# Gated attention after cross-attention on one core: VectorE also turns the odd heads' probability tiles in five of eight rounds, and small products and counts move to GpSimd and ScalarE

## The chip, the cores and the metric

One core of a Trainium2 chip. The metric is the device time of one launch in microseconds (us), given as the median over several runs. TensorE is PE in the rows, VectorE DVE, ScalarE ACT, GpSimd POOL, and SyncE, which issues the transfers, SP.

## The reference, cut to what matters

Two layers over x of shape 8 x 512 x 512 (batch, tokens, width). The first, a cross-attention, gives x1. The second, in which the change lies, works on the normalised x1:

```python
q = (x @ Wq)  # 8 heads of 64;  k = (x @ Wk) likewise
wv = topk_mask(x @ Ws, 2) * sigmoid(x @ Ws)     # per token, head, expert (5)
xv = einsum('btd,edk->btek', x, Wv)
v = einsum('bthe,btek->bhtk', wv, xv)           # values, mixed over experts
probs = softmax(q * scale @ k.T)                # 512 x 512 per head
attn = probs @ v
mask_o = topk_mask(x @ Wd, 2)
out = einsum('bthe,bthk,ekd->btd', mask_o, attn, Wo)
x = x1 + tanh(g) * out
```

## The kernel before, in words

The program has five instruction streams, one per engine, written out by hand; each engine runs its stream in order and waits on semaphores. The second layer (from about 490 us on) takes one batch after another, and a batch goes through **rounds**, numbered n. Rounds 0 to 7 make the scores: heads come in pairs p (an even and an odd one), a pair has two rounds, and a round has four score tiles of 128 queries x 512 keys, in the order even, odd, even, odd head. Preparation of a batch lies in rounds -3 to -1, and its end in rounds 8 to 12. Since a batch's round n + 8 is the next batch's round n, the loop over batches (`Fori`) runs rounds 5 to 12 of batch b, woven with rounds -3 to 4 of batch b + 1. Below, a round is called by its number 5 to 12 in the loop's body; 8 to 12 are then the next batch's 0 to 4.

Within a round each engine goes through the places SCORES, BEFORE, TURNS, BEHIND, AFTER. The table `AT` says at which round and place a unit of matrix work stands: "q", "k", "experts", "turn_y" (transposes of the normalised input), "values" (probs @ v), "turn_o" (turns attn back), "turn_z", "result". All these but "values" share three PSUM banks (`RING`) in the order of the list: a unit waits until the unit three places ahead of it has been read (`wait_bank`, `wait_read`); for "turn_o" of pair p this is when both `mix_product`s of the pair are done.

A score tile goes this way. TensorE makes it (`scores`, L2251); VectorE takes the row maximum (`row_max`, L1860); ScalarE takes the exponential into SBUF (`scores_exp`, L1670). For "values" the tile must be turned. An **even** head's tile is turned in 32 x 32 blocks by VectorE (`turn_blocks`, L1865), and then SP issues four transfers that put the blocks in place in `pt` (`move_blocks`, L1519). An **odd** head's tile is turned by TensorE (`turn_probs`, L2259: four transposes against an identity) and copied from PSUM by ScalarE (`probs_copy`, L1679).

GpSimd mixes the values of each pair (`mix_values`, L1587 and L1593: five products and four sums of 128 x 512) and adds some heads' expert products (`mix_sums`, L1605). Its stream in the loop is `mix_sums(b, 2)`, `mix_values(b + 1, 0)`, then `rest(b + 1)`: the values of pairs 1, 2, 3, and then `mix_sums` of pairs 0 and 1. VectorE makes the products of the attention output with the output gates (`mix_product`, L1879), two heads each in rounds 5, 7, 9 and 10, which need `coef`, the gates over the softmax sums (`coefficients`, L1903, VectorE, rounds 11, 5, 7 and 8). VectorE also ranks the logits in round 8 (`compare`, `count_better`, L1948 to L1960) and copies the norm values (`take_norm`, L1856). `route_values` (round 9) turns the ranks into `pick` and `mask`; `pick` starts the next batch's `mix_values`.

```python
                if a == 0:
                    dve.wait_ge(to_ps, b * PAIRS + p + 1)
                    dve.wait_ge(coef_ready, b * PAIRS + p + 1)
```

These lines head `mix_product`. The last batch ends outside of the loop, in `last_rounds`, where TensorE turns all tiles.

Of the kernel before, what the change touches and what calls it, by code (L numbers as in the profile page):

```python
# [24 lines left out]
ALU = mybir.AluOpType  # L25
# [3 lines left out]
P = 128  # L29
# [1138 lines left out]
def expert_attention(nc, block, both, x1, g_ffn, wk, wo, out):  # L1168
# [29 lines left out]
    BANKS = 4  # L1198
# [32 lines left out]
    COEFFICIENTS_AT = (3, 5, 7, 8)  # L1231
# [38 lines left out]
    with ExitStack() as mem:  # L1270
# [36 lines left out]
        probs_odd = sb("probs_odd", [P, BANKS // 2, T])  # L1307
# [32 lines left out]
        compared = sem("compared")  # L1340
        gates = sem("gates")
# [21 lines left out]
        coef_ready = sem("coef_ready")  # L1363
        z_dve = sem("z_dve")
# [54 lines left out]
        def even_probs(n):  # L1419
            return probs_even[:, n // BANKS % 2, :, n % BANKS // 2, :]  # L1420

        def plain_probs(n):

            if n % 2:
                return probs_odd[:, n % BANKS // 2, :]
            return both.tmp[:, n // BANKS % 2 * 2 + n % BANKS // 2, :]
# [50 lines left out]
        COMPARISONS, GATES = 2 * (E - 1), E + 1  # L1477
# [5 lines left out]
        ODD_STEPS, ODD_ROUND = STEPS // 2, BANKS // 2  # L1483
        MOVED = QUADS * 16
        LAST_TURNED = (B - 1) * ODD_STEPS + (CUT + 1) * ODD_ROUND - (CUT + 1) * BANKS

        def odd_turned(b, n):

            return b * ODD_STEPS + n // 2 + 1

        def all_turned(n):

            return LAST_TURNED + n + 1

# [4 lines left out]
        def _(sp):  # L1499
# [11 lines left out]
            def move_blocks(b, r, first=False):  # L1511

                p = r // 2
                sp.wait_ge(blocks_turned, b * ODD_STEPS + (r + 1) * ODD_ROUND)
                if first and p == 2:

                    sp.wait_ge(o_ps, p - 1)
                for q in range(QUADS):
                    sp.dma_start(by_rows(2 * p % 4)[:, r % 2, q].rearrange("p k s a -> p (k s a)"),  # L1519
                                 probs_even[q * BLOCK:(q + 1) * BLOCK, r % 2].rearrange(  # L1520
                                     "p (j k) s a -> p j (k s a)", j=QUADS)).then_inc(moved[r % 2], 16)
# [43 lines left out]
        def _(pool):  # L1565
# [68 lines left out]
            pool.wait_ge(coef_ready, B * PAIRS)  # L1634
# [5 lines left out]
        def _(act):  # L1640
# [8 lines left out]
            def normalise(b, tiles):  # L1649
                act.wait_ge(norm_ready, b)  # L1650
                act.wait_ge(x1_loaded, b * 16)
# [3 lines left out]

            def scores_exp(b, n, first):
                act.wait_ge(nmax_ready, b * STEPS + n + 1)
                h, t = head_tile(n)
                scores = ps_s[:, n % BANKS, :]
                if n % 2 == 0:  # L1660
                    if n >= 2 * BANKS or not first:

                        act.wait_ge(moved[n // BANKS % 2], (b * PAIRS + n // PAIR) * MOVED)
                    out, scores = even_probs(n), scores.rearrange("p (j a) -> p j a", a=BLOCK)
# [8 lines left out]
            def probs_copy(b, n, first):  # L1673
                h, t = head_tile(n)
                act.wait_ge(pt_ps, odd_turned(b, n))
                if t == 0 and (h >= 4 or not first):

                    act.wait_ge(o_ps, b * PAIRS + h // 2 - 1)
                act.activation(turned(n), scored(n), ACT.Copy).then_inc(pt_ready, 1)  # L1679

            def last_exp(b, n):
                act.wait_ge(nmax_ready, b * STEPS + n + 1)
                h, t = head_tile(n)
                if n % 2 == 0:
                    act.wait_ge(moved[n // BANKS % 2], (b * PAIRS + n // PAIR) * MOVED)
                elif n < STEPS - BANKS:
                    act.wait_ge(pt_ps, odd_turned(b, n - BANKS))
                else:
                    act.wait_ge(pt_ps, all_turned(n - BANKS))
# [55 lines left out]
            def step(b, n, place, first=False):  # L1745
# [18 lines left out]
                elif place == TURNS:  # L1764
# [3 lines left out]
                    if 0 <= n < ROUNDS:  # L1768
# [72 lines left out]
        def _(dve):  # L1841
# [10 lines left out]
            def take_norm(b):  # L1852

                dve.wait_ge(last_newton, ROOT_STEPS + 1)
                dve.wait_ge(y_act, b * NT)
                dve.tensor_scalar(norm[:], x1_norm[:, :, bass.ds(b * NT, NT)], 1.0, None, ALU.mult).then_inc(norm_ready, 1)  # L1856

# [606 lines left out]
```

## Time and profile before

| what | value |
|---|---|
| median of 3 runs | 1152.17 us (1152.14 to 1153.83) |
| the profiled execution | 1152.18 us, span 1150.4 us |
| busy, TensorE | 97% of the span |
| busy, VectorE | 79% |
| busy, ScalarE | 51% |
| busy, GpSimd | 57% |
| granted TensorE clock | 1.00 |

The span goes from the first instruction to the last; 1.8 us lie around it. Busy shares are means over two layers. A row of the timeline reads: start in us, length in us, engine, line, operation, what it writes from what it reads, how many instructions are merged, and in brackets how long the engine was idle before them and what ended the wait.

### The profile page before, as it was taken

How to read it: one execution, taken by the hardware profiler on the slowest of the kernel's cores; microseconds unless marked ns; L12 is line 12 of the kernel's file. 1: busy time of each engine (PE TensorE's matmuls, PEld its weight loads, DVE VectorE, ACT ScalarE, POOL GpSimd, SP SyncE). 2: the span in 40 equal slices, each digit the busy share in tenths (PEclk: the TensorE clock that was granted, in tenths of full speed). 3: DMA queues.
4: the chain of work that ended last, by engine and by line, in shares of the span. 5: the costliest groups of instructions: out<-in, count | busy, mean ns of one | idle time of the engine just before them, and what ended most of it. 6: DMA issues, size and time to landing. Idle time of an engine off the chain costs nothing.

```text
span 1150.4 us, 19136 instructions
## 1 busy us (share of the span) xinstructions
PE 1120.2 (97%) x5885; PEld 856.2 (74%) x5885; DVE 904.9 (79%) x1656; ACT 588.6 (51%) x1332; POOL 658.0 (57%) x476
## 2 busy tenths in 40 slices
PE   7999999999999999999999999999999999999998
PEld 6888888888888888886666767767667666767655
DVE  7998787878787866578597797786887876976977
ACT  7634443434444344447455555555556545565543
POOL 2645252525252524329759579389398498496694
DMA  5441414141414132343324323324225233242241
GB/s 202 147 138 46 138 46 128 55 128 55 128 55 128 55 91 92 129 129 74 91 56 129 88 51 117 91 55 130 71 58 161 55 91 111 55 122 59 55 128 38
DMA packets 76606, 108.44 MB, mean 94 GB/s; under 512 B 7712, under 2 KB 40224, under 8 KB 76576
## 3 DMA queue, kind: packets, MB, share of 16 engines
q1 hardware_dynamic: 76576, 108.07, 31.0%
q8 instruction: 15, 0.25, 0.1%
q14 instruction: 15, 0.12, 0.0%
HBM read 58.76 MB, written 16.78 MB: 66 GB/s over the span
## 4 chain that ended last, share of the span: by engine, by line
PE 68%; POOL 13%; DVE 8%; issue 6%; ACT 4%; DVEq 0%; DMA 0%; POOLq 0%; ACTq 0%; SPq 0%
PE ps_f L992 23%; PE ps_s L992 8%; PE ps_o L2274 7%; PE ps_h L992 7%; POOL spare L1587 6%; PE ps_r L2200 6%; POOL spare L1593 5%; PE ps_r L2233 5%; PE ps_s L2251 4%; PE ps_r L2209 3%; DVE nmax L1860 3%; PE ps_s L2259 2%; DVE z_tmp L1879 2%; ACT probs_odd L1670 1%; POOL z L1605 1%
## 5 line engine op out<-in xcount | busy, mean ns | idle before, releaser
L1860 DVE TENSOR_REDUCE nmax<-ps_s 128x1 f32<-128x512 f32 x256 | 158.5, 680 | 79.0 <-PE ps_s L2251 78.0
L1587 POOL TENSOR_TENSOR spare<-xv,pick 128x512 f32<-128x512 f32 x160 | 184.8, 1155 | 35.0 <-DVE pick L1975 22.1
L1605 POOL TENSOR_TENSOR z<-z,z_tmp 128x1280 f32<-128x1280 f32 x35 | 102.6, 2932 | 138.6 <-DVE z_tmp L1879 136.3
L1593 POOL TENSOR_TENSOR spare<-spare 128x512 f32<-128x512 f32 x128 | 165.6, 1294 | 10.0
L1670 ACT ACTIVATE tmp<-ps_s,nmax 128x512 f32<-128x512 f32 x124 | 85.2, 687 | 97.1 <-DVE nmax L1860 97.1
L2274 PE MATMUL ps_o<-pt,spare 128*64 128x512 f32 x496 | 113.3, 598 | 6.6 <-POOL spare L1593 5.1
L254 POOL TENSOR_TENSOR e_t<-e_t 128x512 fp32r<-128x512 f32 x28 | 35.4, 1300 | 135.7 <-ACT e_t L510 135.7
L2251 PE MATMUL ps_s<-k,q 64*128 64x512 f32 x768 | 106.4, 408 | 3.1 <-ACT pt L1679 3.1
L2251 PEld LDWEIGHTS ps_s<-k,q 64*128 64x128 f32 x768 | 67.3, 184 | 49.3 <-issue 33.3
L254 POOL TENSOR_TENSOR c<-stage,c 128x512 fp32r<-128x512 f32 x28 | 42.3, 1542 | 94.4 <-ACT c L250 94.4
L2200 PE MATMUL ps_r<-es_t,c_t 128*128 128x512 f32 x384 | 96.3, 399 | 0.0
L2200 PE MATMUL ps_r<-es_t,wk 128*128 128x512 f32 x384 | 95.2, 397 | 0.0
L992 PE MATMUL ps_s<-c_t,es_t 128*128 128x512 f32 x384 | 92.8, 393 | 2.4 <-DVE es_t L727 2.4
L992 PE MATMUL ps_f<-wec,e_t 128*128 128x512 f32 x384 | 92.1, 392 | 0.0
L992 PE MATMUL ps_f<-weh,eh_t 128*128 128x512 f32 x384 | 91.9, 391 | 0.0
L992 PE MATMUL ps_f<-wh,h_t 128*128 128x512 f32 x384 | 91.3, 390 | 0.5 <-DVE h_t L887 0.5
L992 PE MATMUL ps_h<-es_t,c 128*128 128x512 f32 x384 | 88.7, 390 | 0.2 <-DVE es_t L781 0.2
L1670 ACT ACTIVATE probs_odd<-ps_s,nmax 128x512 f32<-128x512 f32 x124 | 85.1, 686 | 0.0
L992 PEld LDWEIGHTS ps_s<-c_t,es_t 128*128 128x128 f32 x384 | 71.0, 188 | 17.8 <-DVE es_t L727 2.8
L992 PEld LDWEIGHTS ps_f<-wh,h_t 128*128 128x128 f32 x384 | 72.0, 188 | 15.9 <-DVE h_t L887 0.9
L992 PEld LDWEIGHTS ps_h<-es_t,c 128*128 128x128 f32 x384 | 71.9, 188 | 15.1 <-DVE es_t L781 0.3
L992 PEld LDWEIGHTS ps_f<-wec,e_t 128*128 128x128 f32 x384 | 71.4, 188 | 15.0 <-DVE wec L254 0.4
(245 smaller groups left out, 2272.2 us busy)
## 6 DMA issues: line engine op xcount, KB each, us to landing
pt<-tmp SPq DMA_DIRECT2D x248, 128.0 KB, 2.6
stage<-in_x SPq DMA_DIRECT2D x32, 256.0 KB, 3.2
x_sb<-in_x SPq DMA_DIRECT2D x8, 1024.0 KB, 5.3
x_dram<-x_sb SPq DMA_DIRECT2D x32, 256.0 KB, 3.1
stage<-x_dram SPq DMA_DIRECT2D x8, 1024.0 KB, 5.4
x_sb<-x_dram SPq DMA_DIRECT2D x8, 1024.0 KB, 5.4
out_dram<-x_sb SPq DMA_DIRECT2D x31, 256.0 KB, 2.6
stage<-in_ctx_t SPq DMA_DIRECT2D x28, 256.0 KB, 2.8
```

Source lines behind the costliest of these rows:

```text
L254: return eng.tensor_tensor(pair[:, 1, k, :], operand[:, k, :], pair[:, 0, k, :].bitcast(F32), ALU.subtract)
L992: last = pe.matmul(out, left(l, k), right(r, k), start=start and n == 1, stop=stop and n == ND * len(PASSES))
L1587: pool.tensor_tensor(v_tmp[:] if e else acc, xv[:, :, e, :].unsqueeze(2).broadcast_to(shape), pick[:, e, :, 2 * p:2 * p + 2].unsqueeze(3). ...
L1593: pool.tensor_tensor(acc, acc, v_tmp[:], ALU.add).then_inc(v_steps, 1)
L1605: pool.tensor_tensor(zv, zv, z_tmp[:, h % 2], ALU.add).then_inc(z_pool, 1)
L1670: act.activation(out, scores, ACT.Exp, bias=nmax[:, n:n + 1], accum_out=den[:, h, t:t + 1]).then_inc(p_exp, 1)
L1860: dve.tensor_reduce(nmax[:, n:n + 1], ps_s[:, n % BANKS, :], AX_X, ALU.max, negate=True).then_inc(nmax_ready, 1)
L2200: end = pe.matmul(ps, w2[:, l, k, n * P:(n + 1) * P], y_t2[:, r, k, :], start=m == 0, stop=m == len(every) - 1)
L2209: end = pe.matmul(ps[:, 0:NX], y_t2[:, l, k, n * P:(n + 1) * P], wx2[:, r, k, :], start=m == 0, stop=m == len(every) - 1)
L2233: end = pe.matmul(ps, z_t2[:, zt(l, k), n * P:(n + 1) * P], wo2[:, r, k, :], start=m == 0, stop=m == len(every) - 1)
L2251: end = pe.matmul(ps_s[:, (n + a) % BANKS, :], q2[head_rows(a), p % 2, l, t * P:(t + 1) * P], k2[head_rows(a), p % 2, r, :], start=m == 0, ...
L2274: end = pe.matmul(ps_o[head_rows(a), :], v_acc[:, p, k, a, :], rows, start=k == 0, stop=k == NT - 1)
```

## The change

`ALL_BY_VECTOR` names rounds 0, 4, 5, 6 and 7. In these rounds VectorE turns both heads' tiles, in one instruction for the two tiles of a head (128 x 1024), SP moves both heads' blocks (eight transfers in place of four), and TensorE's transposes and ScalarE's copies of the odd tiles fall away; TensorE's next scores wait for the exponentials there, not for the copies. The odd tiles have two places now, as the even ones.

`coefficients` leaves VectorE for GpSimd (but pairs 2 and 3 of the last batch). It stands in GpSimd's stream between the mixtures: pair 0 behind `mix_values` of pair 2, pair 1 behind `mix_values` of pair 3, pair 2 behind `mix_sums` of pair 1, pair 3 ahead of `mix_sums` of pair 2. The four adds of `count_better` become `rank` on GpSimd, which stands ahead of that. ScalarE makes the copy of the norm values.

```diff
-    COEFFICIENTS_AT = (3, 5, 7, 8)
+
+    ALL_BY_VECTOR = (0, 4, 5, 6, 7)
...
-        probs_odd = sb("probs_odd", [P, BANKS // 2, T])
+        probs_odd = sb("probs_odd", [P, BANKS // 2, T])[:], spare[:, 1, 2:4, :]
...
+        def blocks(r, i):
+
+            if i:
+                return probs_odd[r % 2].rearrange("p s t -> p (s t)").rearrange("p (j s a) -> p j s a", s=2, a=BLOCK)
+            return probs_even[:, r % 2]
...
+                for i in heads_moved(r):
+                    sp.wait_ge(blocks_turned, b * tiles_moved(ROUNDS) + tiles_moved(r) + 2 * i + 2)
+                    if first and p == 2 and i == 0:
+
+                        sp.wait_ge(o_ps, p - 1)
+                    for q in range(QUADS):
+                        sp.dma_start(by_rows((2 * p + i) % 4)[:, r % 2, q].rearrange("p k s a -> p (k s a)"),
+                                     blocks(r, i)[q * BLOCK:(q + 1) * BLOCK].rearrange(
+                                         "p (j k) s a -> p j (k s a)", j=QUADS)).then_inc(moved[r % 2], 16)
...
+            def coefficients(b, p):
+                heads = slice(2 * p, 2 * p + 2)
+                pool.wait_ge(rden_ready, b * PAIRS + p + 1)
+                if p == 0:
+                    pool.wait_ge(mask_ready, b + 1)
+                pool.tensor_tensor(coef[:, heads], mask[:, :, :, heads].rearrange("p e t h -> p h t e"),
+                                   rden[:, heads, :].unsqueeze(3).broadcast_to([P, 2, NT, E]),
+                                   ALU.mult).then_inc(coef_ready, 1)
+
+            def rank(b):
+
+                pool.wait_ge(compared, (b + 1) * COMPARISONS)
+                rows = beaten[:].rearrange("p s k j g -> p (s k) j g")
+                pool.tensor_tensor(better[:], rows[:, :, 0, :], rows[:, :, 1, :], ALU.add).then_inc(ranked, 1)
+                for j in range(2, E - 1):
+                    pool.wait_ge(ranked, b * RANKS + j - 1)
+                    pool.tensor_tensor(better[:], better[:], rows[:, :, j, :], ALU.add).then_inc(ranked, 1)
+                pool.wait_ge(sig_exp, b + 1)
+                pool.wait_ge(ranked, b * RANKS + RANKS - 1)
+                pool.tensor_tensor(logits[:].rearrange("p s k g -> p (s k) g"), better[:], rows[:, :, E - 1, :],
+                                   ALU.add).then_inc(ranked, 1)
+
             def rest(b, first=False):
-                for p in range(1, PAIRS):
-                    mix_values(b, p, first)
+                mix_values(b, 1, first)
+                mix_values(b, 2, first)
+                coefficients(b, 0)
+                mix_values(b, 3, first)
+                coefficients(b, 1)
                 for p in range(LAST_PAIR - 1):
                     mix_sums(b, p)
+                coefficients(b, 2)
...
+            def turn_of(b):
+
+                rank(b + 1)
+                coefficients(b, LAST_PAIR)
+                mix_sums(b, LAST_PAIR - 1)
+                mix_values(b + 1, 0)
+
+            rank(0)
             mix_values(0, 0, True)
             rest(0, True)
             with pool.Fori(0, B - 2) as b:
-                mix_sums(b, LAST_PAIR - 1)
-                mix_values(b + 1, 0)
+                turn_of(b)
                 rest(b + 1)
-            mix_sums(B - 2, LAST_PAIR - 1)
-            for p in range(PAIRS):
-                mix_values(B - 1, p)
+            turn_of(B - 2)
+            mix_values(B - 1, 1)
+            mix_values(B - 1, 2)
+            coefficients(B - 1, 0)
+            mix_values(B - 1, 3)
+            coefficients(B - 1, 1)
...
+                if tiles[0] == 0:
+                    act.wait_ge(last_newton, ROOT_STEPS + 1)
+                    act.activation(norm[:], x1_norm[:, :, bass.ds(b * NT, NT)], ACT.Copy).then_inc(norm_ready, 1)
...
+            def place_free(b, n, first):
+
+                r = n // BANKS
+                if first and r < 2:
+                    return
+                if n % BANKS == 0:
+                    act.wait_ge(moved[r % 2], moved_through(b, r - 2))
+                elif n % 2 not in heads_moved((r - 2) % ROUNDS):
+                    act.wait_ge(pt_ps, odd_turned(b, n - 2 * BANKS))
...
+                if n % 2 in heads_moved(r):
+                    out, scores = blocks(r, n % 2)[:, :, n % BANKS // 2, :], scores.rearrange("p (j a) -> p j a", a=BLOCK)
                 else:
-                    if n >= BANKS or not first:
-
-                        act.wait_ge(pt_ps, odd_turned(b, n - BANKS))
-                    out, scores = plainly(probs_odd[:, n % BANKS // 2, :]), scores_by_keys(scores)
+                    out, scores = plainly(plain_probs(n)), scores_by_keys(scores)
...
+                    if 0 <= n < ROUNDS and n not in ALL_BY_VECTOR:
                         for tile in range(n * BANKS + 1, n * BANKS + BANKS, 2):
                             probs_copy(b, tile, first)
...
-            def turn_blocks(b, n):
-
-                dve.wait_ge(p_exp, b * STEPS + n + 1)
-                dve.transpose(even_probs(n), even_probs(n)).then_inc(blocks_turned, 1)
+            def turn_blocks(b, r, i):
+
+                dve.wait_ge(p_exp, b * STEPS + r * BANKS + i + 3)
+                both_tiles = blocks(r, i).rearrange("p j s a -> p (j s a)")
+                dve.transpose(both_tiles, both_tiles).then_inc(blocks_turned, 2)
...
-            def coefficients(b, p):
+            def last_coefficients(b, p):
                 heads = slice(2 * p, 2 * p + 2)
                 dve.wait_ge(rden_ready, b * PAIRS + p + 1)
-                if p == 0:
-                    dve.wait_ge(mask_ready, b + 1)
                 dve.tensor_tensor(coef[:, heads], mask[:, :, :, heads].rearrange("p e t h -> p h t e"),
                                   rden[:, heads, :].unsqueeze(3).broadcast_to([P, 2, NT, E]),
-                                  ALU.mult).then_inc(coef_ready, 1)
+                                  ALU.mult).then_inc(last_coef, 1)
...
-            def count_better(b):
-
-                dve.wait_ge(compared, (b + 1) * COMPARISONS)
-                rows = beaten[:].rearrange("p s k j g -> p (s k) j g")
-                dve.tensor_tensor(better[:], rows[:, :, 0, :], rows[:, :, 1, :], ALU.add).then_inc(gates, 1)
-                for j in range(2, E - 1):
-                    dve.wait_ge(gates, b * GATES + j - 1)
-                    dve.tensor_tensor(better[:], better[:], rows[:, :, j, :], ALU.add).then_inc(gates, 1)
+            def count_values(b):
                 dve.wait_ge(sig_exp, b + 1)
-                dve.wait_ge(gates, b * GATES + E - 2)
-                dve.tensor_tensor(logits[:].rearrange("p s k g -> p (s k) g"), better[:], rows[:, :, E - 1, :],
-                                  ALU.add).then_inc(gates, 1)
-
-            def count_values(b):
                 dve.tensor_scalar(sig[:], sig[:], 1.0, None, ALU.add).then_inc(gates, 1)
...
+                dve.wait_ge(ranked, b * RANKS + RANKS)
...
-                        for tile in range(n * BANKS, n * BANKS + BANKS, 2):
-                            turn_blocks(b, tile)
+                        for i in heads_moved(n):
+                            turn_blocks(b, n, i)
...
-                    pe.wait_ge(pt_ready, odd_turned(b, n + 1 - BANKS))
+                    if (n // BANKS - 1) % ROUNDS in ALL_BY_VECTOR:
+                        pe.wait_ge(p_exp, b * STEPS + n + 2 - BANKS)
+                    else:
+                        pe.wait_ge(pt_ready, odd_turned(b, n + 1 - BANKS))
...
-                pe.wait_ge(pt_ready, odd_turned(b, PAIR * p + PAIR - 1))
-                for r in range(2):
-                    pe.wait_ge(moved[r], (b * PAIRS + p + 1) * MOVED)
+                if not {2 * p, 2 * p + 1} <= set(ALL_BY_VECTOR):
+                    pe.wait_ge(pt_ready, odd_turned(b, PAIR * p + PAIR - 1))
+                for r in (2 * p, 2 * p + 1):
+                    pe.wait_ge(moved[r % 2], moved_through(b, r))
...
+                    elif place == TURNS and n not in ALL_BY_VECTOR:
                         for tile in range(n * BANKS + 1, n * BANKS + BANKS, 2):
                             turn_probs(b, tile)
```

## Rows read from the trace of the kernel before

**Rows 1.** The page, part 1: busy us, share of the span and instructions.

```profile
PE 1120.2 (97%) x5885; PEld 856.2 (74%) x5885; DVE 904.9 (79%) x1656; ACT 588.6 (51%) x1332; POOL 658.0 (57%) x476
```

**Rows 2.** One period of the loop, rounds 5 to 12: length, busy time by engine.

```profile
700.91:782.12 81.21, 79.46 (x446) 56.37 (x445) 64.75 (x102) 45.96 (x113) 58.48 (x42) 1.00 0.32 90
```

**Rows 3.** The chain that ended last, in order of time, from round 9.

```profile
749.34 1.29 POOL z L1605
...
768.55 3.65 PE ps_o L2274 x16
```

**Rows 4.** Timeline of TensorE, rounds 5 to 7.

```profile
707.64 0.65 PE L2191 MATMUL ps_r<-ident,stage 128*128 128x128 f32 x4 [0.40 <-DVE z_tmp L1879]
...
716.50 1.03 PE L2259 MATMUL ps_s<-ident,probs_odd 128*128 128x128 f32 x8
717.66 4.58 PE L2209 MATMUL ps_r<-c,es_t 128*128 128x400 f32 x24
...
729.75 1.04 PE L2259 MATMUL ps_s<-ident,probs_odd 128*128 128x128 f32 x8
730.72 3.65 PE L2274 MATMUL ps_o<-pt,spare 128*64 128x512 f32 x16
```

**Rows 5.** Timeline of GpSimd, rounds 9 to 7 of the next period.

```profile
749.33 5.92 POOL L1605 TENSOR_TENSOR z<-z,z_tmp 128x1280 f32<-128x1280 f32 x2 [16.15 <-DVE z_tmp L1879]
...
758.84 2.17 POOL L1587 TENSOR_TENSOR spare<-xv,pick 128x512 f32<-128x512 f32 x1
...
762.47 1.05 POOL L1587 TENSOR_TENSOR spare<-xv,pick 128x512 f32<-128x512 f32 x1
...
778.38 1.29 POOL L1593 TENSOR_TENSOR spare<-spare 128x512 f32<-128x512 f32 x1
...
789.57 1.28 POOL L1593 TENSOR_TENSOR spare<-spare 128x512 f32<-128x512 f32 x1
```

**Rows 6.** Timeline of VectorE, round 9, and rounds 12 and 5.

```profile
747.68 2.88 DVE L1879 TENSOR_TENSOR z_tmp<-ps_r,coef 128x1280 f32<-128x1280 f32 x2
...
778.37 1.30 DVE L1865 STREAM_TRANSPOSE tmp<-tmp 128x512 f32<-128x512 f32 x2
...
785.82 1.48 DVE L1879 TENSOR_TENSOR z<-ps_r,coef 128x1280 f32<-128x1280 f32 x1
```

**Rows 7.** Groups of the second layer: busy us, mean ns, idle before.

```profile
L1865 DVE STREAM_TRANSPOSE tmp<-tmp 128x512 f32<-128x512 f32 x124 | 80.1, 682 | 0.0
...
L1903 DVE TENSOR_TENSOR coef<-mask,rden 128x40 f32<-128x40 bf16 x32 | 22.9, 716 | 0.0
...
L1957 DVE TENSOR_TENSOR better<-better,beaten 128x320 bf16<-128x320 bf16 x16 | 5.2, 325 | 0.6
```

**Rows 8.** Timeline of the first batch, round 5: GpSimd, VectorE, and TensorE's round 7.

```profile
546.26 1.27 POOL L1593 TENSOR_TENSOR spare<-spare 128x512 f32<-128x512 f32 x1
...
540.03 1.48 DVE L1879 TENSOR_TENSOR z<-ps_r,coef 128x1280 f32<-128x1280 f32 x1
...
559.75 1.67 PE L2251 MATMUL ps_s<-k,q 64*128 64x512 f32 x12 [2.08 <-ACT pt L1679]
```

**Rows 9.** Timeline of TensorE at the start of the program.

```profile
4.07 4.08 PE L999 MATMUL ps_b<-ident 128*128 128x128 f32 x18 [4.07 <-DVE stats L663]
...
9.79 1.04 PE L999 MATMUL ps_b<-ident 128*128 128x128 f32 x8
```

**Rows 10.** Timeline of the last batch: VectorE, SP's queue, TensorE, GpSimd.

```profile
1110.28 1.48 DVE L1879 TENSOR_TENSOR z<-ps_r,coef 128x1280 f32<-128x1280 f32 x1
...
1115.42 2.50 SPq L1519 DMA_DIRECT2D pt<-tmp  x4
...
1120.07 3.65 PE L2274 MATMUL ps_o<-pt,spare 128*64 128x512 f32 x16 [1.53 <-issue]
...
1128.86 1.95 PE L2301 MATMUL ps_o<-pt,spare 128*64 128x256 f32 x16 [0.84 <-issue]
...
1137.68 1.54 POOL L1619 TENSOR_TENSOR z<-z,pt 128x640 f32<-128x640 f32 x1 [2.85 <-DVE z L2056]
```

More of the change, by code:

```diff
@@ L1474, in head_rows, with heads_moved, tiles_moved, odd_tiles @@
             return slice(a * DH, a * DH + DH)
-        COMPARISONS, GATES = 2 * (E - 1), E + 1
+        COMPARISONS, RANKS, GATES = 2 * (E - 1), E - 1, 2
         V_STEPS = 2 * E - 1
-        ODD_STEPS, ODD_ROUND = STEPS // 2, BANKS // 2
-        MOVED = QUADS * 16
-        LAST_TURNED = (B - 1) * ODD_STEPS + (CUT + 1) * ODD_ROUND - (CUT + 1) * BANKS
+        def heads_moved(r):
+            return range(2 if r in ALL_BY_VECTOR else 1)
+        def tiles_moved(r):
+            return sum(2 * len(heads_moved(i)) for i in range(r))
+        def odd_tiles(n):
+            return sum(m // BANKS not in ALL_BY_VECTOR for m in range(1, n + 1, 2))
+        def transfers(r):
+            return sum(QUADS * 16 * len(heads_moved(i)) for i in range(r % 2, r + 1, 2))
+        def moved_through(b, r):
+            earlier = r < 0
+            return b * transfers(ROUNDS - 2 + r % 2) + transfers(r + ROUNDS * earlier) - earlier * transfers(
+                ROUNDS - 2 + r % 2)
         def odd_turned(b, n):
-            return b * ODD_STEPS + n // 2 + 1
+            earlier = n < 0
+            return b * odd_tiles(STEPS - 1) + odd_tiles(n + STEPS * earlier) - earlier * odd_tiles(STEPS - 1)
         def all_turned(n):
-            return LAST_TURNED + n + 1
+            return (B - 1) * odd_tiles(STEPS - 1) + odd_tiles((CUT + 1) * BANKS - 1) + n + 1 - (CUT + 1) * BANKS
         POOL_SUMS, LAST_PAIR = H - 3, PAIRS - 1
@@ L1513, in move_blocks @@
                 p = r // 2
[L1514 to L1521, printed above, removed]
+                for i in heads_moved(r):
[6 more added lines that the diff above has]
+                                         "p (j k) s a -> p j (k s a)", j=QUADS)).then_inc(moved[r % 2], 16)
             def steady(b, more):
@@ L1658, in scores_exp @@
                 h, t = head_tile(n)
[L1659 to L1664, printed above, removed]
-                else:
-                    if n >= BANKS or not first:
-                        act.wait_ge(pt_ps, odd_turned(b, n - BANKS))
-                    out, scores = plainly(probs_odd[:, n % BANKS // 2, :]), scores_by_keys(scores)
+                r, scores = n // BANKS, ps_s[:, n % BANKS, :]
+                place_free(b, n, first)
+                if n % 2 in heads_moved(r):
+                    out, scores = blocks(r, n % 2)[:, :, n % BANKS // 2, :], scores.rearrange("p (j a) -> p j a", a=BLOCK)
+                else:
+                    out, scores = plainly(plain_probs(n)), scores_by_keys(scores)
                 act.activation(out, scores, ACT.Exp, bias=nmax[:, n:n + 1],
@@ L1675, in probs_copy @@
                 act.wait_ge(pt_ps, odd_turned(b, n))
-                if t == 0 and (h >= 4 or not first):
+                if n % BANKS == 1 and (h >= 4 or not first):
                     act.wait_ge(o_ps, b * PAIRS + h // 2 - 1)
@@ L1683, in last_exp @@
                 h, t = head_tile(n)
[L1684 to L1689, printed above, removed]
+                place_free(b, n, False)
                 act.activation(plainly(plain_probs(n)), scores_by_keys(ps_s[:, n % BANKS, :]), ACT.Exp, bias=nmax[:, n:n + 1],
@@ L1985, in step @@
                 if place == SCORES:
-                    if n == NORMALISE_AT and not first:
-                        take_norm(b)
                     for p in range(PAIRS):
@@ L2080, in last_rounds @@
                     row_max(b, n)
-                coefficients(b, 2)
+                last_coefficients(b, 2)
                 for h in (2, 3):
@@ L2088, in last_rounds @@
                 row_sums(b, 3)
-                coefficients(b, 3)
+                last_coefficients(b, 3)
                 last_mix(5, turned_pair(2))
@@ L2246, in scores @@
                 elif n >= BANKS or not first:
-                    pe.wait_ge(pt_ready, odd_turned(b, n + 1 - BANKS))
+                    if (n // BANKS - 1) % ROUNDS in ALL_BY_VECTOR:
+                        pe.wait_ge(p_exp, b * STEPS + n + 2 - BANKS)
+                    else:
+                        pe.wait_ge(pt_ready, odd_turned(b, n + 1 - BANKS))
                 for m, (l, r) in enumerate(PASSES):
```

25 lines of the change are left out of this document (9 added, 16 removed).

## The prediction

> **What bounds the kernel now.** I read the busy shares first, then the chain that ended last, then the timelines of one period. TensorE is busy 97% of the span, and in a period of the second layer 79.5 of 81.2 us [rows 1, 2]. So five rounds without its transposes look like pure gain. The chain says something else beside it: in round 9 it enters GpSimd's sums, stays on GpSimd over the whole mixture of pair 0, and comes back to TensorE when "values" of pair 0 may start, 19 us later [rows 3]. GpSimd is busy only 58.5 of the 81.2 us [rows 2], but between round 9 and round 7 its stream has no free time. Whatever is queued into that stretch is paid in full by whoever waits for it. The second thing to see is that TensorE's second turn_y of round 5 waits 0.40 us for VectorE's products [rows 4]: it needs the bank that `mix_product` of heads 0 and 1 must have read. TensorE has no lead over these products.
>
> **The change, part by part.**
>
> *TensorE.* The turning of a round's two odd tiles takes, from its start to the next unit's, 1.16 us in round 6 and 0.97 in round 7 [rows 4]; I take 1.0 for the others. Five rounds are 5.0 us a period; 38 rounds are changed in all (8 batches by 5, less rounds 6 and 7 of the last), 38 us.
>
> *VectorE.* Two more tiles cost 1.3 us a round (0.68 each, 1.30 for two) [rows 6, 7], 6.5 us a period. Four coefficients at 0.72 [rows 7], four counts at 0.33 or a little more [rows 7], together 4.3 us, and a small norm copy go. Net some +2 us on 64.8 busy of 81.2 [rows 2]: it is covered by VectorE's waits.
>
> *ScalarE* loses ten copies and gains one tiny one; at 46 of 81 us busy [rows 2] it doesn't matter.
>
> *GpSimd, coefficients.* This is the step that decides. `coefficients(b, 0)` now stands behind `mix_values` of pair 2. In the timeline of before, the stream that starts with the sums at 749.33 ends the mixture of pair 2 at 789.57 + 1.28 = 790.85 [rows 5]. But VectorE uses this coefficient at 785.82, in round 5 [rows 6]. It will wait. The price of the coefficient itself is not in the trace: GpSimd takes 1.54 us for 640 elements and 2.9 for 1280 [rows 5, 10], so 2.1 ns an element and 0.2 fixed, which gives 0.3 us for 40; bounds are 0.1 (elements alone) and 1.05 (a whole product of 512). With 0.1 to issue it and 0.2 for the signal to VectorE, as from VectorE to GpSimd (the second product of round 9 starts half way through the 2.88 us from 747.68, and so the first ends at 749.12; the sums start at 749.33) [rows 5, 6] product 0 starts at 791.4 instead of 785.8: **5.6 us late**, 4.9 us if the coefficient is free, 6.4 if dear.
>
> Nothing hides it. VectorE stands at product 0, behind it the low part of k for pair 3, the round's block turns and all later row maxima; TensorE stands at the second turn_y. GpSimd's stretch starts with the products of round 9, so this is a closed loop. From the end of round 9's first product (749.12) to product 0: 36.7 us before, 42.3 after. From product 0 to the first product's end in round 9: 749.12 - (785.82 - 81.2) = 44.5 us before [rows 2, 6]. Of that, round 6 gives 1.16 and round 7 gives 0.97; round 8 is VectorE's (it trades 0.2 of coefficient and 1.5 of counts for 1.3 of turns), so 0.4 to 0.5. The savings of rounds 12 and 5 (some 0.85 each) lie ahead of the wait and only make it longer. Period: 42.3 + 44.5 - 2.6 = 84.2, **3.0 us more than before** (81.2), not 5.0 less.
>
> *GpSimd, counts.* Four adds of 320 by the same line are 0.85 each, with gaps 3.9 us, while VectorE has some 4.4 us of other work between the comparisons and `pick` (four row maxima, the low part of q, the reciprocal). I cost it at nothing. At the price of a whole 512 (1.29) [rows 5] it would be about 1 us late, and with a dear coefficient behind it, which `mask` waits for, 2 us a period. The Trainium skill, GPSIMD Engine Reference, section Engine selection, says that elementwise work belongs on VectorE, GpSimd being about twice as slow; by that factor on the trace's 0.325 us the four adds take 2.6 us and are hidden too.
>
> *Port.* When VectorE adds two SBUF operands, a GpSimd product takes 2.17 us for the usual 1.05; beside VectorE's block turns a GpSimd sum keeps its 1.29 [rows 5, 6]. So I add nothing for more turns beside the mixtures. If they did collide, two such rounds would lie in the stretch, 2 to 4 us a period. The Trainium skill, SBUF — State Buffer, section Who interferes with whom, has the same line between one SBUF input and two.
>
> *Transfers.* Eight in place of four a round: four are issued in 2.50 us, and "values" starts 2.15 us after the last [rows 10]. In the loop a round is 8 to 12 us and `pt` is needed a round or more later, so it is hidden; if it weren't, 2.5 us a round. At the end it isn't hidden (below).
>
> *TensorE after the wait.* TensorE reaches the second turn_y earlier by rounds 12 and 5 and waits longer: 5.6 + 0.4 + 1.7, so 7.7 us in one piece. The trace has one wait that long or near it, 4.07 us at the program's start, and behind it 18 transposes take 4.08 us (0.227 each), where 8 later take 1.04 (0.130), though the granted clock reads 1.00 in all rows; a wait of 2.08 us in the first batch slows nothing (12 score products 1.67 us) [rows 8, 9]. The start may be slow for another reason. I take it as the same thing, since 7.7 is well past 4.07: 4.08 - 18 x 0.130 = **1.74 us** lost behind each such wait, on the path. With none it is 0; with half speed through the following "values" (3.65 us) as well, 3.6. The Trainium skill, TensorE: Matmul & The Clock Gate, Part 1, says that an idle TensorE falls from 2.4 to 1.2 GHz and must be busy again before it gets the clock back; by that rule the loss is certain, which speaks against this change.
>
> *The ends.* First batch: the mixture of pair 2 ends at 547.53, product 0 stood at 540.03 [rows 8], so 8.1 us late; less 1.0 for round 0's turning, ahead of it. Less 2.6 as above and 2.1, because TensorE's wait in round 7 (2.08, which came from the end of the mixtures) goes: +2.4 us. Last batch: 5.6 late, then "values" of pair 2 wait for round 5's eight transfers. Product 0 to "values" was 1120.07 - 1110.28 = 9.8; it becomes 2.8 + 0.6 + 1.2 (products, k, first turn) + 5.0 + 2.15 = 11.8: +2.0; and 0.84 of wait for the last mixture goes [rows 10]: +6.8.
>
> *Sum.* 2.4 + 6 periods x 3.0 + 6.8 = 27.2; eight slow restarts x 1.74 = 13.9; together 41 us on the profiled execution's 1152.2 (span 1150.4 and 1.8 around it), which is the median too. **1193 us.**
>
> **The rivals.**
>
> *Clock stays (22%).* The start is slow for its own reason. Then 1152.2 + 27.2 = 1179.
>
> *GpSimd's small work is dear (12%).* Counts and coefficient at the upper bounds, 2.3 us more a period: 7 x 2.3 = 16, so 1209. For it: no row has a GpSimd operation of this size or of bf16. Against: the line through 640 and 1280 has a small fixed part.
>
> *The wait is partly absorbed (9%).* The mixtures run faster with fewer two-input operations of VectorE beside them (the two 2.17 us products at 1.05 would give 2.2 us a period), and TensorE's clock stays: 1179 - 7 x 2.2 = 1164; up to a third of this case comes out within 0.2% of 1152.
>
> *Faster (8%).* The late coefficient holds VectorE only, and TensorE runs on through the order of the banks, so that its own work sets the time: 1152 - 38 = 1114. It needs the wait at product 0 to cost the loop less than the 2.6 us that rounds 6, 7 and 8 give back. Against it are the 0.40 us wait at turn_y and that the product is read in place from one of three banks. For it: TensorE's 97%.
>
> *Worse than all (4%):* round 9 and the transfers add to the wait, 1215 or more.
>
> The forecast with waits and slow restarts has 45%.
>
> **Range and chances.** 1172 to 1210 takes in the clock rival, the bounds of the coefficient (5 us each way) and the dear case to its centre. A difference under 0.2% can't be told from none here. Slower 45 + 22 + 12 + 6 + 4 = 89%, same 3%, faster 8%.
>
> **What the changed profile would show.** VectorE's product 0 in round 5 idle before by several us, released by GpSimd's coefficient; TensorE idle before the second turn_y of every round 5, 7 to 8 us, released by product 1; periods of 84 us (86 with slow restarts, and then longer "values" behind the wait); GpSimd's mixtures unchanged; ranks done before `pick`. Wrong would be: product 0 without idle time, periods under 81, counts over 1 us each, or turns that stretch GpSimd's products.

## The result, and the profile after

The changed kernel takes **1205.6 us** (median of 4 runs, 1204.2 to 1205.9) beside 1152.7 of the kernel before on the same chip: ratio 1.0456, 95% interval 1.0441 to 1.0472. It is slower, as forecast; 1193 was forecast, with a range of 1172 to 1210.

The busy row and the row of the granted clock of its page, beside [rows 1]:

```profile
PE 1106.2 (92%) x5581; PEld 828.6 (69%) x5581; DVE 911.5 (76%) x1563; ACT 553.2 (46%) x1263; POOL 689.0 (57%) x538
PEclk9999999999999999997998998999989989989989
```

TensorE has 304 matmuls less to do and is 14 us less busy, in a span 54 us longer: it waits. Here are TensorE, VectorE and GpSimd in round 5, the place of [rows 4, 6]; each fence is one engine's timeline.

```profile
719.02 0.66 PE L2234 MATMUL ps_r<-ident,stage 128*128 128x128 f32 x4 [0.67 <-ACT stage L1716]
726.48 1.11 PE L2234 MATMUL ps_r<-ident,stage 128*128 128x128 f32 x4 [6.81 <-DVE z_tmp L1937]
727.52 6.15 PE L2321 MATMUL ps_o<-pt,spare 128*64 128x512 f32 x16
```
```profile
723.47 1.49 DVE L1937 TENSOR_TENSOR z<-ps_r,coef 128x1280 f32<-128x1280 f32 x1 [6.62 <-POOL coef L1636]
```
```profile
721.75 1.26 POOL L1617 TENSOR_TENSOR spare<-spare 128x512 f32<-128x512 f32 x1
723.09 0.27 POOL L1636 TENSOR_TENSOR coef<-mask,rden 128x40 f32<-128x40 bf16 x1
723.32 2.18 POOL L1611 TENSOR_TENSOR spare<-xv,pick 128x512 f32<-128x512 f32 x2
```

Read it from the bottom. A coefficient of 0.27 us stands behind the last sum of a mixture of 11 us (712.02 to 723.01). VectorE's product 0 has waited 6.62 us for it, and TensorE's second turn_y 6.81 us for the second product of VectorE. And the "values" behind that wait take 6.15 us where they take 3.65 in [rows 4]. The windows of this stretch (length; busy time of TensorE, its loads, VectorE, ScalarE, GpSimd; then the granted clock) say why:

```profile
719.00:723.00 4.00, 0.66 (x4) 0.42 (x4) 0.00 (x0) 3.04 (x5) 3.77 (x4) 0.92 0.54 208
723.00:725.00 2.00, 0.00 (x0) 0.00 (x0) 1.53 (x2) 0.00 (x0) 1.84 (x4) 0.50 0.64 190
...
729.00:731.00 2.00, 2.00 (x8) 0.48 (x5) 1.51 (x4) 0.00 (x0) 1.84 (x3) 0.50 0.60 145
731.00:733.00 2.00, 2.00 (x8) 0.61 (x6) 0.00 (x0) 0.00 (x0) 1.84 (x3) 0.60 0.78 202
733.00:735.00 2.00, 2.00 (x16) 1.05 (x12) 0.40 (x1) 0.60 (x1) 1.92 (x3) 1.00 0.69 177
```

During the wait the granted clock falls from 1.00 to 0.50, from 2.4 to 1.2 GHz, and it is back only when "values" are nearly done. It does so in all eight batches, and these "values" take 4.6 to 6.2 us. (By the Trainium skill, TensorE: Matmul & The Clock Gate, Part 1, this had to follow an idle stretch; the trace agrees, with 0.92 in the stretch in which TensorE stops and 0.50 in the next.)

GpSimd's new small work in round 8 answers [rows 7]:

```profile
763.55 0.79 POOL L1644 TENSOR_TENSOR better<-beaten 128x320 bf16<-128x320 bf16 x1 [8.35 <-DVE beaten L2004]
764.42 1.67 POOL L1647 TENSOR_TENSOR better<-better,beaten 128x320 bf16<-128x320 bf16 x2
766.17 0.79 POOL L1650 TENSOR_TENSOR logits<-better,beaten 128x320 f32<-128x320 bf16 x1
...
769.89 2.92 POOL L1629 TENSOR_TENSOR z<-z,z_tmp 128x1280 f32<-128x1280 f32 x1 [2.69 <-DVE z_tmp L1937]
```

The counts end at 766.96 and `pick` starts at 767.80, so they are hidden, and GpSimd waits another 2.69 us before its sums. The end, beside [rows 10] (TensorE, then SyncE's queue). TensorE waits twice. The first wait is for the low part of k, which VectorE writes behind its products until 1164.90; the second is for round 5's transfers:

```profile
1165.00 2.93 PE L2297 MATMUL ps_s<-k,q 64*128 64x512 f32 x12 [4.92 <-issue]
...
1173.26 5.15 PE L2321 MATMUL ps_o<-pt,spare 128*64 128x512 f32 x16 [4.28 <-issue]
```
```profile
1166.08 2.50 SPq L1543 DMA_DIRECT2D pt<-tmp  x4
1168.63 2.58 SPq L1543 DMA_DIRECT2D pt<-spare  x4
```

**Where the 53.6 us of span went.** Product 0 of round 5 marks each batch. Before it starts at 540.03 in the first batch, at 623.42 in the second and at 1110.28 in the last; after at 547.44, 635.34 and 1161.41. The first batch is 7.4 us later there, the first period 4.5 us longer (83.4 to 87.9), the six periods of the loop 39.2 us (81.1 to 87.7 each, +6.5), and the stretch from the last product 0 to the end 2.5 us (40.1 to 42.6). The forecast in the same parts is 7.1, 2.6, 28.4 and 2.9.

### The profile page after: what moved, and what is told of

It reads as the page before. It is cut to its first block, busy times and chain, and to the rows that moved or that the text cites. A ratio compares the mean times of both kernels' runs of the same rounds, so it can differ in the third digit from the quotient of the medians.

```text
span 1204.0 us, 18434 instructions
## 1 busy us (share of the span) xinstructions
PE 1106.2 (92%) x5581; PEld 828.6 (69%) x5581; DVE 911.5 (76%) x1563; ACT 553.2 (46%) x1263; POOL 689.0 (57%) x538
## 4 chain that ended last, share of the span: by engine, by line
PE 57%; POOL 21%; DVE 10%; issue 7%; ACT 3%; POOLq 1%; DVEq 0%; DMA 0%; ACTq 0%; SPq 0%
PE ps_f L992 22%; POOL spare L1611 11%; POOL spare L1617 9%; PE ps_s L992 7%; PE ps_h L992 6%; PE ps_o L2321 6%; PE ps_r L2243 4%; PE ps_r L2252 3%; PE ps_s L2297 3%; DVE nmax L1917 2%; DVE z_tmp L1937 2%; ACT probs_odd L1738 1%; POOL z L1629 1%; DVE beaten L2004 1%; ACT tmp L1738 1%
## 5 line engine op out<-in xcount | busy, mean ns | idle before, releaser
L1738 ACT ACTIVATE tmp<-ps_s,nmax 128x512 f32<-128x512 f32 x124 | 85.4, 688 | 120.3 <-DVE nmax L1917 120.3
L2321 PE MATMUL ps_o<-pt,spare 128*64 128x512 f32 x496 | 127.4, 661 | 9.4 <-POOL spare L1617 5.1
L2297 PEld LDWEIGHTS ps_s<-k,q 64*128 64x128 f32 x768 | 68.4, 186 | 52.5 <-issue 39.6
L2321 PEld LDWEIGHTS ps_o<-pt,spare 128*64 128x64 f32 x496 | 36.4, 152 | 81.8 <-issue 75.0
L2252 PE MATMUL ps_r<-c,es_t 128*128 128x400 f32 x384 | 75.3, 348 | 7.0 <-DVE es_t L1969 7.0
```

The source lines that it names most:

```text
L1738: act.activation(out, scores, ACT.Exp, bias=nmax[:, n:n + 1], accum_out=den[:, h, t:t + 1]).then_inc(p_exp, 1)
L2252: end = pe.matmul(ps[:, 0:NX], y_t2[:, l, k, n * P:(n + 1) * P], wx2[:, r, k, :], start=m == 0, stop=m == len(every) - 1)
L2297: end = pe.matmul(ps_s[:, (n + a) % BANKS, :], q2[head_rows(a), p % 2, l, t * P:(t + 1) * P], k2[head_rows(a), p % 2, r, :], start=m == 0, ...
L2321: end = pe.matmul(ps_o[head_rows(a), :], v_acc[:, p, k, a, :], rows, start=k == 0, stop=k == NT - 1)
```

## The experiments

All stand beside the kernel before on the same chip, and each compares with the changed kernel unless told otherwise. The table has the time, its ratio with the interval, the mean of the six loop periods and the first one (product 0 to product 0), and the time from the last product 0 to the end.

| kernel | median us | ratio to before | period | first | end |
|---|---|---|---|---|---|
| before | 1152.7 | | 81.1 | 83.4 | 40.1 |
| after | 1205.6 | 1.0456 (1.0441 to 1.0472) | 87.7 | 87.9 | 42.6 |
| x1 early coefficient | 1139.8 | 0.9885 (0.9869 to 0.9902) | 78.8 | 82.8 | 45.9 |
| x2 TensorE kept busy | 1193.2 | 1.0341 (1.0324 to 1.0358) | 85.4 | 87.3 | 44.4 |
| x3 no odd turns | 1210.2 | 1.0499 (1.0482 to 1.0517) | 88.6 | 88.2 | 39.6 |
| x4 turns only | 1153.3 | 1.0004 (0.9994 to 1.0013) | 80.6 | 82.5 | 45.1 |
| x5 = x1, counts on VectorE | 1155.0 | 1.0011 (1.0001 to 1.0021) | 80.6 | 81.6 | 45.9 |
| x6 = x1, all eight rounds | 1162.2 | 1.0075 (1.0058 to 1.0092) | 81.9 | 83.2 | 45.4 |
| x7 = x1, no odd turns | 1159.4 | 1.0047 (1.0030 to 1.0063) | 81.1 | 86.9 | 45.6 |
| x8 = x1, rounds 0, 4, 7 | 1149.8 | 0.9966 (0.9952 to 0.9981) | 79.8 | 86.0 | 45.9 |
| x9 = x1, rounds 0, 4, 6, 7 | 1140.5 | 0.9890 (0.9874 to 0.9907) | 78.7 | 83.1 | 47.3 |

(x1's parts are those of its repetition x11: 1139.1 us, 0.9881, 0.9864 to 0.9897. In x1's own profiled execution they are 78.7, 81.5 and 46.1. Each row's parts are of one execution, so a difference of 1 us in "first" says nothing. That of x9 took 1.9 us more than its median.)

**x1, the order alone.** `coefficients(b, 0)` goes one mixture earlier, in the loop and in the last batch:

```diff
                 mix_values(b, 1, first)
+                coefficients(b, 0)
                 mix_values(b, 2, first)
-                coefficients(b, 0)
                 mix_values(b, 3, first)
```

> The changed kernel with one thing moved: GpSimd makes the coefficients of pair 0 behind the mixture of pair 1, not of pair 2. If the late coefficient is the cause, product 0 of round 5 no longer waits, TensorE's 6.8 us wait in round 5 and the slow stretch behind it go, and the next limit is the end of GpSimd's mixtures (experts of the next batch may be written only then): a period of 77 to 78 us in place of 88.4, total 1120 to 1132. If the turns on VectorE or the eight transfers are the cause, the time stays near 1205.

Measured 1139.8, 66 us less than after and 13 less than before; the period is 78.8. The cause is as expected; the time is 8 us above the expected 1120 to 1132. TensorE in round 5:

```profile
699.60 1.41 PE L2234 MATMUL ps_r<-ident,stage 128*128 128x128 f32 x8 [0.67 <-ACT stage L1716]
700.93 3.65 PE L2321 MATMUL ps_o<-pt,spare 128*64 128x512 f32 x16
...
710.37 4.59 PE L2252 MATMUL ps_r<-c,es_t 128*128 128x400 f32 x24 [1.00 <-DVE es_t L1969]
```

The 6.8 us wait is gone and so is the slow stretch. The whole loss was the place of one 0.27 us instruction. What misses of the expected gain stands in the same rows, 0.67 us behind ScalarE's casts and 1.00 at the low part of y (`es_t`), and at the end, where 45.9 us follow the last product 0 instead of 40.1. TensorE waits there 6.50 us for round 5's transfers (first row, the timeline of x11), and it is tempting to name these. The chain of x11 at that place (second fence: start, length, what) says otherwise:

```profile
1106.61 6.04 PE L2321 MATMUL ps_o<-pt,spare 128*64 128x512 f32 x16 [6.50 <-issue]
```
```profile
1108.81 1.05 POOL spare L1611
...
1109.93 1.28 POOL spare L1617
...
1111.28 0.28 POOL coef L1636
...
1111.65 0.10 DVE z_tmp L2078
```

VectorE waits 7.81 us for the last batch's `coefficients(B - 1, 1)`, behind the mixture of pair 3: the same fault a second time, one pair later. It lies over the wait for transfers. In the loop nothing else took the coefficient's place: the chain of x11 goes from round 9's products over GpSimd's sums and the mixture of pair 0 to "values" (978.70 to 997.95, 19.2 us), as in [rows 3].

**x2, the wait without the fall of the clock.** TensorE does 56 transposes that nobody reads while it would wait:

```diff
+                if (name, n) == ("turn_y", 1):
+                    pe.wait_ge(p_exp, b * STEPS - STEPS + (CUT + 1) * BANKS)
+                    for _ in range(56):
+                        pe.transpose(ps_s[:, 0, 0:P], ident[:], ident[:])
```

> The changed kernel with 56 idle transposes on TensorE (0.11 us each, 6.2 us, into a score bank that is free) ahead of the second turn_y of round 5, where it waits 6.8 us for product 0. The wait itself stays. If the slow values (5.4 to 6.2 us for 3.65) behind it come from the idle time, they go back to 3.65, the granted clock is 1.00 again, and 7 periods get 2.5 to 3 us shorter: 1184 to 1190, a little less if the 1.0 us wait at experts goes too. If they come from something else (the transfers, the turns), the time stays at 1205 or gets worse.

Measured 1193.2, a gain as expected and 3 us short of its range. VectorE's wait is still 6.61 us, but the granted clock is 1.00 from 715 to 730 and behind the idle work "values" take 3.65 again:

```profile
716.10 6.28 PE L2233 MATMUL ps_s<-ident 128*128 128x128 f32 x56
723.06 0.65 PE L2238 MATMUL ps_r<-ident,stage 128*128 128x128 f32 x4 [0.68 <-DVE z_tmp L1937]
723.64 3.65 PE L2325 MATMUL ps_o<-pt,spare 128*64 128x512 f32 x16
```

So of the 6.5 us that a period has more, the low clock is 2.3 (87.7 less 85.4) and the rest, 4.3, is the late product less what the turns give. The first and the last batch have waits that the idle work doesn't fill (3.98 us behind it in the first), and stayed slow: "values" take 5.09 and 6.42 us there.

**x3, without the turns.** `ALL_BY_VECTOR = ()`, all else as in the change.

> The changed kernel without its turns: no round is turned by VectorE alone; coefficients and counts stay on GpSimd and the norm copy on ScalarE, at the changed places. If the moves alone set the time, product 0 waits as in the changed kernel (about 5.6 us), TensorE idles about 6 us and is slow behind it: a period of 88 to 90 us, 1200 to 1215. If the turns have a part in the loss, it lies clearly under 1200; if they are the whole loss, at 1150.

Measured 1210.2, period 88.6, as the first case has it:

```profile
727.23 1.11 PE L2234 MATMUL ps_r<-ident,stage 128*128 128x128 f32 x4 [5.87 <-DVE z_tmp L1937]
728.27 5.10 PE L2321 MATMUL ps_o<-pt,spare 128*64 128x512 f32 x16
```

The wait belongs to the moved coefficient and not to VectorE's turns or the transfers. Under the late coefficient the turns are worth 0.9 us a period (88.6 to 87.7). The 1.0 us wait for the low part of y, once a batch in the changed kernel (7.0 us in seven waits), does not exist here, so it comes with the turns; x9 shows with which.

**x4, the turns alone.** Coefficients and counts back on VectorE, where they were; the norm copy stays on ScalarE.

```diff
+    COEFFICIENTS_AT = (3, 5, 7, 8)
...
             def coefficients(b, p):
+                return
...
             def rank(b):
 
+                return
...
+                    if n in COEFFICIENTS_AT:
+                        coefficients(b, COEFFICIENTS_AT.index(n))
...
                         compare(b)
+                        count_better(b)
```

The two returns empty GpSimd's functions; VectorE has its own again.

> The turns alone: odd heads' tiles on VectorE in five rounds and the norm copy on ScalarE as changed, but coefficients and counts back on VectorE at their old places. If the turns are worth their 5 us of TensorE a period where nothing waits for GpSimd, the period is limited by the longer VectorE work of round 8 and by GpSimd's mixtures: about 79 us, 1130 to 1140. If VectorE becomes the bound (67 to 70 us of work) or the transfers hold up, 1150 or more.

Measured 1153.3, no difference from before: **the expected 1130 to 1140 was wrong**, and its other case, VectorE as the bound, came out. TensorE is busy 4 us a period less than before (75.39 us from 702.75 to 783.33, against 79.46 in [rows 2]), but the period is only 0.5 shorter. VectorE waits for nobody from 736 to 762, in rounds 8 and 9, where the counts lie:

```profile
736.93 1.20 DVE L1926 STREAM_TRANSPOSE probs_odd<-probs_odd 128x1024 f32<-128x1024 f32 x1
738.05 1.93 DVE L2016 TENSOR_TENSOR beaten<-logits 128x256 bf16<-128x256 f32 x8
740.01 0.33 DVE L2022 TENSOR_TENSOR better<-beaten 128x320 bf16<-128x320 bf16 x1
740.37 0.68 DVE L2025 TENSOR_TENSOR better<-better,beaten 128x320 bf16<-128x320 bf16 x2
```

Its row maxima come late, so do ScalarE's exponentials, and TensorE waits at its odd tiles in round 9 (timeline, the same place one period on):

```profile
825.18 0.66 PE L2332 MATMUL ps_s<-ident,spare 128*128 128x128 f32 x4 [1.17 <-ACT spare L1741]
826.52 0.73 PE L2332 MATMUL ps_s<-ident,spare 128*128 128x128 f32 x4 [0.68 <-ACT spare L1741]
827.19 5.22 PE L2348 MATMUL ps_o<-pt,spare 128*64 128x512 f32 x16
```

Here nothing lies over the transfers at the end, and the chain shows 6.46 us of waiting for them and then "values" of 5.54 us: product 0 to the end is 5 us longer than before, and that eats what the loop gave.

**x5, x1 with the counts back on VectorE** (`rank` empty, `count_better` behind `compare`; the coefficients stay on GpSimd).

> Coefficients of pair 0 made early on GpSimd, turns as changed, and the four counts back on VectorE (1.5 us in round 8, ahead of pick, mask and product 4). If round 8 and 9 of VectorE are on the loop that sets the period, each period grows from 78.75 by about 1.5 us to 80.2: 1148 to 1152. If the counts on GpSimd were hidden either way, nothing changes: 1140.

Measured 1155.0, 3 us above the expected range, and the period is 80.6, as in x4. Beside x1 the counts on GpSimd are worth 1.8 us a period and 15 us in all. x4 and x5 differ in who makes the coefficients, and the period is the same: moving these is worth nothing here, although the coefficients are 0.86 us each on VectorE in x4. TensorE's waits for the exponentials of the odd tiles, in x5 (first) and in x11 (second; us in total, times, longest):

```profile
PE ps_s L2319 <- ACT spare L1739: 16.7, 20, 1.4
```
```profile
PE ps_s L2305 <- ACT spare L1738: 6.4, 15, 0.6
```

A count takes GpSimd 0.79 us and VectorE 0.33 [rows 7], and still it belongs on GpSimd, which waits at that place, while VectorE has nothing free. (The Trainium skill, GPSIMD Engine Reference, section Engine selection, puts elementwise work on VectorE because GpSimd is about twice as slow; the price agrees with the runs, 0.79 to 0.33, the advice does not hold in a round where VectorE is full.)

**x6, x1 with all eight rounds by VectorE.** `ALL_BY_VECTOR = (0, 1, ..., 7)`.

> Coefficients of pair 0 early on GpSimd, and all eight rounds turned by VectorE. TensorE loses another 3 us of work a period, VectorE gains 3.6 us in rounds 9 to 11, where it has hardly a wait. If TensorE's work set the period it would fall to 76 and the total to 1120. If the loop over VectorE's round 9 and GpSimd's mixture of pair 0 sets it, the period stays within 1 us of 78.75: 1135 to 1147.

Measured 1162.2, **wrong again**, above both of its cases, for the same reason: in rounds 9 and 10 VectorE has no wait left, and its sum of z comes late to turn_z. TensorE's waits for it:

```profile
PE ps_r L2266 <- DVE z L1948: 35.6, 7, 5.1
```

**x7, x1 with no odd turns.** `ALL_BY_VECTOR = ()`.

> Coefficients of pair 0 early on GpSimd, counts on GpSimd, norm copy on ScalarE, and no round turned by VectorE alone: the moves without the turns. VectorE has 4.3 us less a period, 1.7 of it in round 8 where it led TensorE by little. If that is on the loop, the period falls from 81.2 to about 80.3: 1144 to 1148; the turns are then worth 1.5 us a period, of the 5.0 that TensorE is spared. If the moves are worth nothing by themselves, 1152.

Measured 1159.4, above both cases, period 81.1: the moves alone are worth nothing in the loop. What is lost lies in the first batch (86.9) and at the end (45.6, though TensorE waits but 1.2 us for transfers here; the chain runs over GpSimd's mixtures and the late coefficient as in x1). In the first batch ScalarE waits with the logits until the last mixture is done, and the copies of round 6's odd tiles stand behind them; with round 6 turned by VectorE no copy is there. ScalarE, then TensorE:

```profile
558.86 0.24 ACT L1788 ACTIVATE logits<-ps_r 128x80 f32<-128x80 f32 x1 [7.16 <-POOL spare L1617]
...
559.32 1.09 ACT L1747 ACTIVATE pt<-ps_s 128x512 f32<-128x512 f32 x2
```
```profile
559.97 2.93 PE L2297 MATMUL ps_s<-k,q 64*128 64x512 f32 x12 [3.37 <-ACT pt L1747]
```

**x8, x1 with rounds 0, 4 and 7.** It was to keep the gain and spare the end its transfers.

> Coefficients of pair 0 early on GpSimd, and only rounds 0, 4 and 7 turned by VectorE. In round 6 TensorE's saving of 1.16 us is followed by a wait of 1.0 for the low part of y, in round 5 its 0.87 by a wait of 0.67 for ScalarE, so turning these two back costs about 0.4 us a period; at the end of the last batch the wait for round 5's transfers (6.5 us) and the slow values behind it (2.9 us) go. Sum: 1140 + 3 - 8 = 1135, 1130 to 1138. If the turns of rounds 5 and 6 do pay in full, 1145 or more.

Measured 1149.8, far from the expected 1135, as in the case that the turns pay in full: the first period is 86.0, close to x7's, each loop period 1.1 longer than x1's, and the end is as long as x1's although round 5 moves half the blocks there. With x7 it says that fewer transfers don't shorten x1's end. The loop period grows by what x7 showed in the first batch: TensorE's scores wait for ScalarE's copies of round 6 (some 1.0 us a period, 4.4 in the first batch), which stand behind the logits and so behind GpSimd's last mixture.

```profile
PE ps_s L2297 <- ACT pt L1747: 11.2, 9, 4.4
```

**x9 to x12, which rounds, and the norm copy.** x11 repeats x1. x9 turns rounds 0, 4, 6 and 7. x12 is x1 with ScalarE's norm copy ahead of round 5's exponentials, x10 has both edits.

> The kernel of x1 once more, on the same chip as the three that follow, so that they can be compared with it: 1138 to 1141 us by any theory.

> The early coefficient with rounds (0, 4, 6, 7) by VectorE. Three rounds (0, 4, 7) cost 10 us against five (0, 4, 5, 6, 7): 5 us of it in the first batch, where the odd tiles' copies of round 6 stand on ScalarE behind its wait for the logits, and 1 us a period in the loop. Theory A: round 6 carries all of that, so without round 5 the time stays within 2 us of x1's 1140, and the last batch, with fewer copies waiting, may give 1 to 3 us back: 1137 to 1141. Theory B: each round left out costs its own 0.5 us a period and nothing comes back at the end: 1143 to 1147.

> In x1 TensorE waited 0.67 us a period at the second turn_y for ScalarE, whose norm copy stands between round 5's exponentials and its casts of the mixture. Theory A: that 0.22 us copy, moved ahead of the exponentials, brings the casts 0.2 us earlier and the period from 78.75 to some 78.5: 1136 to 1139 us. Theory B: the casts are held by the exponentials and the scores before them, the copy only moves the exponentials back, and the time stays at 1138 to 1141.

> Both edits. With theory A of both: 1134 to 1139 us; with theory B of both it equals the kernel with four rounds alone, 1143 to 1147.

Measured 1139.1, 1140.5, 1140.0 and 1139.9, with ratios of 0.988 to 0.989 whose intervals (0.986 to 0.991) overlap: nothing tells them apart. Round 6 carries the difference between x8 and x9, and leaving out round 5 changes nothing, so theory A of x9 held. x9 also shows what the two waits of x1 belong to. The 0.67 us for ScalarE is gone there: it had taken back most of what round 5's transposes gave TensorE. The 1.0 us for the low part of y is still there, and x8, without round 6, has none: it belongs to round 6. VectorE does not write this part late because of its turns. It waits for ScalarE, which stands at round 6's exponentials, while TensorE without its transposes comes 1.16 us sooner. TensorE's waits and VectorE's row, of x9:

```profile
PE ps_r L2252 <- DVE es_t L1969: 7.0, 7, 1.0
```
```profile
711.78 1.29 DVE L1969 TENSOR_TENSOR es_t<-ps_r,es_t 128x512 fp32r<-128x512 f32 x2 [1.63 <-ACT es_t L1780]
```

Theory B of x12 held: with the copy earlier turn_y waits 0.34 us for ScalarE and then 0.41 for VectorE's product, where it waited 0.64 for ScalarE in one piece. Of x10's two expectations neither fits, since one edit went by A and the other by B.

```profile
780.97 0.65 PE L2238 MATMUL ps_r<-ident,stage 128*128 128x128 f32 x4 [0.41 <-DVE z_tmp L1941]
```

## Why the prediction was right, and where its sizes were off

The measured 1205.6 lies in the range, 12.6 us above the forecast. It is nearer to the 1209 of the rival with dear small work, but that is chance: that rival's prices were not there.

- **The late coefficient, right.** From the end of round 9's first product to product 0 the prediction has 42.3 us; it is 42.2 (769.67 to 811.86). x1 shows that this place, and nothing else of the change, makes it slower.
- **The counts hidden, and their price, right** (0.79 for 0.85; the coefficient 0.27 for 0.3). The rival with dear small work falls. One of its bounds was worked out wrongly: with a free coefficient product 0 would be 5.3 us late by the prediction's own terms, not 4.9, so that side of the range had 2 us and not 5.
- **The slow restart was there, but mis-sized:** 1.74 us in the sum, 2.3 by x2. The row of the program's start was the wrong measure: the granted clock reads 1.00 there, so that this stretch is slow for a reason that no run shows, and here the clock stays low through the following "values", 4.6 to 6.2 us for 3.65. The upper bound of 3.6 is half speed through "values" alone, without the 1.74 that its words add; the dearest wait in the loop cost 3.0 (0.46 at the transposes, 2.50 at "values"). The wait of 7.7 us came as 7.5 in two pieces, 0.67 for ScalarE's casts and 6.81. The rival in which the clock stays falls.
- **What TensorE gets back behind product 0 was mis-sized.** The prediction takes 2.6 us off for rounds 6, 7 and 8. In x2, without the low clock, the period is 85.4 and not 84.2: TensorE waits 1.0 us at experts for the low part of y, which waits for ScalarE in round 6, and that eats most of round 6's 1.16 (x3, x8 and x9). The step that failed is that TensorE's saved time comes back in full although its next operand comes no sooner.
- These two terms are 0.6 and 1.2 us in each of six periods, 10.8 of the 12.6 us that the forecast lacks. In the first period the miss is 1.9; the two ends came out within 0.4.
- **"Net +2 us on VectorE, covered by its waits" was wrong as a step,** though it cost the forecast nothing, since a longer wait lay over it. VectorE's waits lie elsewhere: in rounds 8 and 9 it has none. x4 and x5 show it. "38 us less on TensorE" is therefore no measure of what the turns can give either: the 1114 of the rival "faster" was not reached by removing the wait. With it removed (x1) the kernel gains 13 us.
- The turns and the counts' move work only together. From x7's 81.1, the turns of rounds 0, 4, 5, 6 and 7 give 2.4 us a period; from before's 81.1 (x4) they give 0.5.
- **Transfers,** hidden in the loop and not at the end: right for the changed kernel, where TensorE has one wait for them, the 4.28 us at the end, and product 0 to "values" takes 11.85 us (1161.41 to 1173.26) and 11.8 was forecast. The forecast left out `coefficients(B - 1, 1)`. In the changed kernel that cost nothing, since VectorE waits 1.74 us for it and the transfers lie over that; it shows once the first coefficient is early.

Left open: that an earlier place for this second coefficient gives x1 its 5 us at the end back was argued from the chain and from x7, and was not tried. By x4 the transfers are late next, at about the same price, so that both would have to be mended.

## What to carry to other kernels

Before a small instruction is moved to an engine with free time, look at what stands ahead of it there and when its reader wants it: 0.27 us of work cost 66 us here, because an 11 us block was ahead of it and the block itself started from the reader's own engine. Look for free time in the round in which the work would lie, not in the engine's share of the span. And when TensorE is relieved, ask which engine makes its next operand in that same round: the gain came only when VectorE had been relieved there too.

## What the runs showed of the hardware

TensorE's clock can fall behind waits much shorter than the 6.8 us here. In x4 two waits of 1.17 and 0.68 us with four transposes between them were followed by 5.22 us for "values" in one period (the rows above), and by 3.65 in another with the same two waits (744.62 and 745.96). The granted clock of the slow one is still 1.00 in both waits. It falls at about 827, when TensorE is busy again:

```profile
824.00:826.00 2.00, 0.67 (x5) 0.42 (x4) 2.00 (x4) 2.00 (x7) 0.00 (x0) 1.00 0.11 32
826.00:828.00 2.00, 1.48 (x6) 0.72 (x8) 1.87 (x4) 1.93 (x5) 0.00 (x0) 0.74 0.00 0
828.00:830.00 2.00, 2.00 (x8) 0.67 (x6) 2.00 (x3) 0.00 (x0) 1.41 (x1) 0.50 0.00 0
830.00:832.00 2.00, 2.00 (x12) 0.47 (x8) 1.66 (x3) 0.00 (x0) 1.92 (x2) 0.90 0.00 0
```

What decides between the two was not settled.

VectorE turns two tiles in one instruction (128 x 1024) in 1.20 to 1.24 us, where two single ones of 0.68 take 1.30 [rows 6, 7].
